# 64-token attention in a float32 network on one core: three one-pass products for q, k and v, and the turned tiles of a layer's last lane issued earlier

## The reference, cut to what matters

```python
def _layer(x, wqkv, qs, ksc, wo, lg, lb, w1, b1, w2, b2):
    h = shift_token(x)                  # upper half of the features moved one token on
    q, k, v = jnp.split(h @ wqkv, 3, axis=-1)         # 128 -> 3 x 512, 8 heads of 64
    q = l2norm(q) * qs
    k = l2norm(k) * ksc
    q, k = rotary_xpos(q, k)
    o = local_attention(q, k, v)        # windows of 64 tokens, each sees itself and the one before
    x = x + o @ wo
    h = layernorm(shift_token(x))
    a, g = jnp.split(h @ w1 + b1, 2, axis=-1)
    return x + (a * gelu(g)) @ w2 + b2
```

## Time and profile before

| | |
|---|---|
| median of the 3 runs | 2840.59 us |
| the profiled execution's own time | 2833.55 us |
| its span | 2831.8 us |
| PE busy | 2659.5 us (94%) |
| DVE, ACT, POOL busy | 1939.5, 1858.8, 1051.8 us (68, 66, 37%) |
| chain that ended last | PE 73%, DVE 11%, ACT 7% |
| granted PE clock, mean | 0.978 |
| the four layers of stage W | 1758.8 to 2225 us and 2360.7 to 2825 us |

### The profile page before, as it was taken

The page is one execution under the profiler, slowest core; times in us unless marked ns, Lnnn a source line. Parts: engine busy times, 40 slices in busy tenths (PEclk is TensorE's granted clock), DMA queues, the critical chain, the costliest instruction groups (busy, mean ns, idle before and its releaser), DMA issues.

```text
span 2831.8 us, 63348 instructions
## 1 busy us (share of the span) xinstructions
PE 2659.5 (94%) x24036; PEld 1812.7 (64%) x24036; DVE 1939.5 (68%) x5616; ACT 1858.8 (66%) x4392; POOL 1051.8 (37%) x876
## 2 busy tenths in 40 slices
PE   8999999999999998899999998998898998998998
PEld 5666656548888885588888885455455563553554
DVE  5555646488788786788888886774675326764774
ACT  5666766626676673478787876776776515875875
POOL 2323323313333330355555552553454013552551
PEclk8999999999999998999999999999999999999999
DMA  1010000000000001000000002210210002111210
GB/s 56 1 43 1 13 1 9 5 9 2 3 2 2 2 2 50 30 2 2 2 2 2 2 2 92 62 45 7 61 49 20 24 1 69 47 30 30 49 42 16
DMA packets 35280, 63.13 MB, mean 22 GB/s; under 512 B 11526, under 2 KB 15654, under 8 KB 33830
## 3 DMA queue, kind: packets, MB, share of 16 engines
q1 hardware_dynamic: 34982, 59.07, 7.5%
HBM read 23.48 MB, written 1.15 MB: 9 GB/s over the span
## 4 chain that ended last, share of the span: by engine, by line
PE 73%; DVE 11%; ACT 7%; issue 3%; SPq 2%; POOL 1%; DMA 1%; DVEq 0%; ACTq 0%; POOLq 0%
PE bank L804 63%; PE bank L1033 5%; PE bank L1153 3%; SPq L770 2%; PE bank L880 1%; ACT low L1364 1%; DVE low L1708 1%; DVE low L1686 1%; ACT work L1400 1%; ACT work L1303 1%; DVE halves L1701 1%; DMA work<-work 1%; DVE work L1588 1%; ACT squared L1275 1%; ACT bank L1279 1%
## 5 line engine op out<-in xcount | busy, mean ns | idle before, releaser
L1271 ACT ACTIVATE low<-bank 128x512 f32<-128x512 f32 (+3 forms) x512 | 427.8, 946 | 0.0
L804 PE MATMUL bank<-table_keys,halves 128*128 128x512 f32 (+3 forms) x1536 | 418.0, 380 | 1.1 <-ACT low L1364 1.0
L804 PE MATMUL bank<-work 128*64 128x128 f32 (+6 forms) x4480 | 364.2, 290 | 39.7 <-DVE work L1795 20.7
L804 PEld LDWEIGHTS bank<-work 128*64 128x64 f32 (+3 forms) x4480 | 265.0, 144 | 211.5 <-issue 147.5
L1364 ACT ACTIVATE low<-bank,low 128x512 f32<-128x512 f32 (+23 forms) x384 | 227.2, 592 | 248.9 <-DVE low L1708 245.4
L1708 DVE TENSOR_REDUCE low<-bank 128x1 f32<-128x512 f32 (+22 forms) x512 | 286.4, 569 | 96.2 <-PE bank L804 91.3
L1898 POOL TENSOR_TENSOR halves<-squared,const 128x512 fp32r<-128x512 f32 x128 | 137.0, 1070 | 510.7 <-PE bank L804 510.7
L1271 ACT ACTIVATE work<-bank 128x512 f32<-128x512 f32 (+4 forms) x389 | 199.5, 538 | 151.2 <-PE bank L804 76.9
L804 PEld LDWEIGHTS bank<-table_keys,halves 128*128 128x128 f32 x1536 | 243.6, 190 | 47.6 <-issue 13.3
L1400 ACT ACTIVATE work<-work 128x192 f32<-128x192 f32 (+1 forms) x512 | 218.7, 431 | 38.2 <-DVE work L1788 38.2
L1947 POOL TENSOR_TENSOR work<-work 128x768 f32<-128x768 f32 x128 | 187.7, 1466 | 135.2 <-DVE work L1799 135.2
(11 more groups left out here) (201 smaller groups left out, 5707.3 us busy)
## 6 DMA issues: line engine op xcount, KB each, us to landing
work<-work SPq DMA_DIRECT2D x512, 64.0 KB, 2.0
slot<-in_wW SPq DMA_DIRECT2D x4, 1605.5 KB, 6.7
slot<-in_wA SPq DMA_DIRECT2D x4, 837.0 KB, 6.4
table_low<-embv_padded SPq DMA_DIRECT2D x2, 1536.0 KB, 6.3
table<-in_dft SPq DMA_DIRECT2D x1, 3072.0 KB, 11.8
slot<-in_wE SPq DMA_DIRECT2D x2, 584.0 KB, 3.7
const<-in_const SPq DMA_DIRECT2D x1, 1094.5 KB, 5.2
squared<-in_x SPq DMA_DIRECT2D x4, 256.0 KB, 6.2
```

Of the source, the lines that this page charges most:

```text
L804: return pe.matmul(o, l, r, start=start, stop=stop)
L1271: return act.activation(dst, src, ACT.Identity)
```

## The change

It does the following.

- q, k and v are now each the sum of three one-pass products: rounded weight times rounded input, rounded weight times the input's rest, and the weight's rest times the rounded input. `w_rotate` and `w_value` issue three `mm` in place of one.
- A new step `w_halves` on POOL, once per layer, makes `W_HI` (copy) and `W_LO` (subtraction) from each of the three 128x512 weights. It stands at the start of each stage W, and for the second layer between the MLPs of lanes 1 and 2 of the layer before.
- A new step `w_split` on POOL, once per lane, makes the rounded input and its rest in `XS` (two buffers). Lane 0's stands right behind its shift, lane 1's in the middle of the head, lane 2's and 3's behind W(j) at the fourth step of lanes 0 and 1.
- `XS` lies in `table_keys`, over the place of the DFT tables; so their load moves from the start of the first stage W to the end of the attention of its second layer (`tables`, which=3).
- In the last lane, from its second step on, `w_turn` of j-1 stands right behind the exponentials of j: PE goes S(j), T(j-1), V(j-2), and DVE goes mask and maximum of j, D(j-1), R(j).

```diff
@@ stage_w
         weights()
+        add("w_halves")
         if seen.get("shift", 0) == 0:
             add("tables", which=2)
-        for c in range(C):
+        add("shift", c=0, via="norm")
+        add("w_split", c=0)
+        for c in range(1, C):
             add("shift", c=c, via="norm")
...
                 if 1 <= j <= lane_items:
                     length(j - 1)
+                if j == lane_items // 2:
+                    add("w_split", c=1)
...
                 if j < len(pairs):
                     add("w_exps", c=lane, i=i, hp=hp)
+                turned = (c >= C - 1 and at > 0)
+                if turned and j <= len(pairs):
+                    lane, i, hp = pairs[j - 1]
+                    add("w_turn", c=lane, i=i, hp=hp)
                 if 2 <= j <= len(pairs) + 1:
...
                     add("w_weigh", c=lane, i=i, hp=hp)
+                if at == 3 and c + 2 < C:
+                    add("w_split", c=c + 2)
                 if c + 1 < C and at in (3, 4, 5, 6):
                     add("w_value", c=c + 1, i=at - 3)
-                if 1 <= j <= len(pairs):
+                if not turned and 1 <= j <= len(pairs):
...
             state["pool"] = range(BANKS)
+            if seen["tables"] == 3 and layer == DEPTH_W - 1:
+                add("tables", which=3)
             add("shift", c=3, via="stream")
...
             if layer < DEPTH_W - 1:
                 weights()
+                add("w_halves")
                 add("shift", c=0, via="stream")
+                add("w_split", c=0)
                 add("w_mlp", c=2, load=load)
...
@@ storage
+        tail = WORK_W - LOW - 6 * T
+        W_HI, W_LO = (halves[:, tail + a * 3 * T:tail + (a + 1) * 3 * T].rearrange("p (x f) -> p x f", x=3) for a in range(2))
+        XS = table_keys[:, 0:4 * T].rearrange("p (l a t) -> p l a t", l=2, a=2)
@@ SP, tables
-                else:
+                elif s.which == 2:
                     sp.wait_ge(sem("r_head_copied"), 2 * BATCHES)
                     sp.dma_start(table[:, 6144:8192], ins["rotary"]).then_inc(sem("rotary_loaded"), 16)
+                else:
+                    sp.wait_ge(sem("w_v_copied"), NT * C * DEPTH_W)
+                    sp.wait_ge(sem("w_squared"), 2 * PAIRS * C * DEPTH_W)
                     sp.dma_start(table[:, 0:6144], ins["dft"]).then_inc(sem("dft_loaded"), 16)
@@ PE, w_rotate
-                pe.wait_ge(sem("shift_done"), C * s.shift + s.c + 1)
-                mm(take(s.k)[:, :], wt(s, WW, s.x, s.pt * P, P), shifted[:, s.c, :]).then_inc(tile_full, 1)
+                layer = s.n // (2 * PAIRS * C)
+                x = "qkv".index(s.x)
+                pe.wait_ge(sem("w_split"), 2 * (C * layer + s.c + 1))
+                pe.wait_ge(sem("w_halved"), 6 * layer + 2 * x + 2)
+                o, mine = take(s.k)[:, :], slice(s.pt * P, s.pt * P + P)
+                mm(o, W_HI[:, x, mine], XS[:, s.c % 2, 0, :], stop=False)
+                mm(o, W_HI[:, x, mine], XS[:, s.c % 2, 1, :], start=False, stop=False)
+                mm(o, W_LO[:, x, mine], XS[:, s.c % 2, 0, :], start=False).then_inc(tile_full, 1)
@@ PE, w_value: the same with XS as the stationary side, 128 columns of it, and W_HI, W_LO moving
@@ POOL
+            def w_halves(s):
+                layer = s.n
+                if layer == 0:
+                    pool.wait_ge(sem("r_head_copied"), 2 * BATCHES)
+                else:
+                    pool.wait_ge(sem("w_v_copied"), NT * C * layer)
+                reached(pool, "w_added", s.rotations)
+                for x, name in enumerate("qkv"):
+                    whole = wt(s, WW, name)
+                    pool.tensor_copy(W_HI[:, x, :], whole).then_inc(sem("w_halved"), 1)
+                    pool.wait_ge(sem("w_halved"), 6 * layer + 2 * x + 1)
+                    pool.tensor_tensor(W_LO[:, x, :], whole, whole_words(W_HI[:, x, :]), ALU.subtract).then_inc(sem("w_halved"), 1)
+                pool.wait_ge(sem("w_halved"), 6 * layer + 6)
+
+            def w_split(s):
+                reached(pool, "w_v_copied", NT * (s.n - 1 if s.c > 1 else s.n - s.c))
+                reached(pool, "w_added", s.rotations)
+                pool.wait_ge(sem("shift_done"), C * s.shift + s.c + 1)
+                pool.tensor_copy(XS[:, s.c % 2, 0, :], shifted[:, s.c, :]).then_inc(sem("w_split"), 1)
+                pool.wait_ge(sem("w_split"), 2 * s.n + 1)
+                pool.tensor_tensor(XS[:, s.c % 2, 1, :], shifted[:, s.c, :], whole_words(XS[:, s.c % 2, 0, :]), ALU.subtract)\
+                    .then_inc(sem("w_split"), 1)
+                pool.wait_ge(sem("w_split"), 2 * s.n + 2)
```

More of the change, by code:

```diff
@@ L604, in hybrid_network @@
         small_w = carve(4, 12)
+        tail = WORK_W - LOW - 6 * T
+        assert cursor[0] <= LOW + tail
+        W_HI, W_LO = (halves[:, tail + a * 3 * T:tail + (a + 1) * 3 * T].rearrange("p (x f) -> p x f", x=3) for a in range(2))
+        XS = table_keys[:, 0:4 * T].rearrange("p (l a t) -> p l a t", l=2, a=2)
         HW = work[:, PAIRS * T:PAIRS * T + 2 * HT_W * T].rearrange("p (a b c) -> p a b c", a=2, b=HT_W)
@@ L1131, in w_value @@
             def w_value(s):
-                mm(take(s.k)[:, :], shifted[:, s.c, s.i * P:(s.i + 1) * P], wt(s, WW, "v")).then_inc(tile_full, 1)
+                layer = s.n // (NT * C)
+                pe.wait_ge(sem("w_split"), 2 * (C * layer + s.c + 1))
+                pe.wait_ge(sem("w_halved"), 6 * layer + 6)
+                o, mine = take(s.k)[:, :], slice(s.i * P, s.i * P + P)
+                mm(o, XS[:, s.c % 2, 0, mine], W_HI[:, 2, :], stop=False)
+                mm(o, XS[:, s.c % 2, 0, mine], W_LO[:, 2, :], start=False, stop=False)
+                mm(o, XS[:, s.c % 2, 1, mine], W_HI[:, 2, :], start=False).then_inc(tile_full, 1)
             def w_scores(s):
@@ L1465, in tables @@
             def tables(s):
-                if s.which == 2:
+                if s.which >= 2:
                     return
@@ L1958, in h_forward @@
                 pool.tensor_tensor(YH[:, b, 1, :], M1[:, b, 1, :], M2[:, b, 0, :], ALU.add).then_inc(sem("h_product"), 1)
-            parts = dict(weights=lambda s: weights_here(pool, s), norm_scale=norm_scale, shift=shift, gate=gate, core=core, a_weigh=a_weigh, w_weigh=w_weigh, w_add=w_add, h_forward=h_forward)
+            parts = dict(weights=lambda s: weights_here(pool, s), norm_scale=norm_scale, shift=shift, w_halves=w_halves, w_split=w_split, gate=gate, core=core, a_weigh=a_weigh, w_weigh=w_weigh, w_add=w_add, h_forward=h_forward)
             pool.wait_ge(sem("const_loaded"), 16)
```

## The result

The changed kernel takes **2860.44 us** in the median of six runs (2846.7 to 2870.62); the kernel before took 2843.67 us in six (2834.72 to 2847.97). The ratio is **1.007**, with an interval of 1.0044 to 1.0096. I had forecast 2841.3 us, no change, in a range of 2824 to 2857: the kernel is slower, by 0.7%, and the time lies outside the range.

A forecast was written before the change was run, and what follows sets the result against it. PE was taken to bound only the main part, loops of waits the head and last lane. Terms -18.4 - 0.5 + 3.2 + 2.8 + 2.4 + 11.2 = +0.7 us on 2840.6 gave 2841.3 us, range 2824 to 2857.

The forecast's parts named there:

- One-pass products, -18.4: Main parts: 144 projections and values each fall by 0.16 us, 23.0 us, of which 80% arrives: -18.4 us.
- Rivals C and D: Product passes: C, each takes 0.86 us, +220 us, chance 0.01; D, quicker passes, some 6 us less, chance 0.08.
- Lane 0's split, +3.2: Start of each stage W: the split delays PE 2.0 us, less 0.4 saved on the first product, twice: +3.2 us.
- lane 1's, +2.8: Head: a 2.0 us split behind an add makes the next add 0.7 us late, four times: +2.8 us.
- lanes 2 and 3, +2.4: Main part: splits between W(j) and the next add cost 0.3 us for each of eight: +2.4 us.
- Rival B: Main part: POOL is late, splits delaying add, scale and ACT; 2.0 us a split, sum +21, 2862 us; chance 0.21.
- w_halves, the DFT load, 0: Start of stage W and between layers: 6 us of halves stay hidden, cover 2 us; the moved table load costs nothing.
- T ahead of V, +11.2: Last lane: T waits for POOL's W, two steps take 6.97 us in place of 6.10; +2.8 us a layer, +11.2 us.
- Rival A: Last lane: the reordering is free or gains; 2830 us, or 2821 us with half the waits recovered; chance 0.25.
- Its eight projections hang on the loop of swap, add and scale, not on PE: 0.: Head: cheaper projections there save no time, since a loop of waits and not PE sets the pace: 0 us.
- if PE's clock falls in the longer gaps, +16: Last lane: upper bound of the reordering's cost, should PE's granted clock fall in its longer gaps: +16 us.
- 7.0 us under the median: Base of the forecast: the profiled execution took 2833.55 us, 7.0 us under the median, so 2840.6 us was used.

The follow-up runs named there:

- e1: The changed kernel with the last lane back in its old order (V before T), all else kept; 2842.94 us, ratio to before 1.0012.
- e3: The changed kernel with the old last-lane order and old float32 products, POOL making halves and splits nobody reads; 2843.32 us, ratio to before 1.0029.
- e2: The kernel before with the last lane's reordering (T ahead of V) and nothing else; 2854.01 us, ratio to before 1.0068.
- e10: The changed kernel with the old last-lane order and two needless float32 products before V(30) in each last lane; 2830.44 us, ratio to before 0.9949.
- e9: The kernel before with two needless float32 products before V(30) in each last lane, nothing else; 2829.11 us, ratio to before 0.9943.
- e5: The changed kernel with the old last-lane order and lane 0's projections and values as float32 products, without its split; 2836.18 us, ratio to before 0.9978.
- e6: The changed kernel with the old last-lane order and lane 0's products given a needless repeat of their first pass; 2838.41 us, ratio to before 0.9991.

## Why the prediction was wrong, point by point

- **One-pass products, -18.4: the size of one product was right, the share that arrives was too high.** 0.89 us a projection against 0.90 forecast, 0.14 us less a value against 0.16. At full clock the first main part gains 3.5 us of 36 x 0.16 = 5.8 us, 60% where I took 80%. Rivals C and D (dearer and quicker passes) fall with these rows. The parts at equal clock say the same: e1 less e3 is -14.6 us, 63% of 23.0.
- **Lane 0's split, +3.2, lane 1's, +2.8, lanes 2 and 3, +2.4.** PE starts 2.1 us later at each of two stages, as forecast, and its first two projections take 2.90 us in place of 3.56. But in e3 the four main parts take 520.3 us (520.1 before) and the heads 112.9 (112.0): in the main part a split costs nothing, in the head 0.2 us a layer in place of 0.7. All of POOL's work is +2.4 us at equal clock; I had 8.4. Rival B (POOL late in the main part, 2862 us) gives the measured time to 2 us by luck: e3 shows its mechanism false.
- **w_halves, the DFT load, 0.** Right: hidden with 1.75 us to spare in the view above, where I had 2.
- **T ahead of V, +11.2.** The loop was right: T 1.78 us behind R, as forecast (R at 1939.47, T at 1941.25), V at once behind T, and POOL as the new releaser. The size is 4.3 us in the first layer's lane, not 2.8. The starts of R give the parts: the first reordered step 1.3 us longer (forecast 1.0), the six behind it 3.0 (forecast 2.6), and the 0.6 us that I gave back at the end did not come (5.6 us from R(31) to the output in either order, at full clock). Four lanes alone are +14.3 us. Rival A (0.25) falls with e2: the reordering is a loss.
- **The sum at an equal clock comes out near** (+2.3 against +0.7), but by luck, since errors cancel: +3.8 on the products, -6.0 on POOL, +3.1 on T.
- **The step that failed is the one on PE's time off the path: "Its eight projections hang on the loop of swap, add and scale, not on PE: 0."** What PE no longer does there was put at nothing, and part of it comes out of the granted clock. The sum had no term for the clock at all; it stood only in a bound of the reordering ("if PE's clock falls in the longer gaps, +16"), and e2 shows 0.001 there. In its place the runs show: the mean fell from 0.975 to 0.967, at 2.28 us per 0.001 some 18 us, which is what the means differ by (20.6) less the 2.3 at equal clock. The one-pass products account for 0.005 to 0.006 of it (e1 against e3, e10 against e9), 12 to 13 us; lane 0's alone, whose projections that sentence is on, for about 0.003 (e5 and e6 against e1), 7 us. POOL's work has 0.001 (e3). Which of the other lanes' products cost the rest, and whether the reordering adds to it once the products are cheap, stays open. A row to start from was before me: the head at 0.87 in the earlier trace rows, the only stretch of the layer well under full clock, with PE busy for 21.7 of 26.0 us.
- **"7.0 us under the median"** was the same thing: the profiled execution had 0.978, 0.003 above the mean of its kernel, 6.9 us on the line.

What stays open: why less busy time in lane 0 also goes with a lower clock at places 100 us later (1.2 GHz behind the last lanes of e1, whose order is that of before). Each profile is one execution, and behind the last lanes the slow stretches do not fall at the same places in each, so these runs do not settle it; only those at the end of the heads stand clear. They too are rarer where the last lanes have the fillers (1.00, 0.81, 1.00 and 1.00 in e10, at the same places as above), and that is as little explained. Not tried either: the old products in lanes 1 to 3 alone, and lane 0's old product with the reordering left in.

## What to carry to other kernels

Time taken from PE where it already waited gained nothing here and was paid for with the clock, so price it by the granted clock of its stretch and of the dense work behind it. Where PE must wait and dense work follows, a needless product placed inside that wait can be worth more than a cheaper product, as here (0.9943 for e9 alone, 1.0012 for e1): try it alone on the kernel before, or its gain is credited to something else. Before an operation is moved ahead of another to end a wait, list what the other one covered (here POOL's 1.47 us under V).

## What the runs showed of the hardware

- The mean granted clock decides between executions of one kernel: the changed kernel's six lie between 2846.7 us at 0.973 and 2870.62 us at 0.963. On the line through them, the clock's 0.010 are 22.8 of these 23.9 us. Most of a difference of 0.3% between executions is this, and it can be read beside each time.
- Eight needless products (two float32 128x512 ones in each of four last lanes, 1.88 us busy a pair) make the kernel before 16 us faster (0.9943).
- POOL's copy of 128x512 took 0.61 us at the start of the stage (shown above), but 1.13 us in the head, where DVE's scale ran beside it; the changed kernel there:

```profile
1777.35 0.69 DVE L1813 SCALAR_TENSOR_TENSOR work<-squared,work 128x512 f32<-128x512 f32 x1 [0.38 <-POOL work L2011]
...
1777.38 1.13 POOL L1930 CAST table_keys<-shifted 128x512 fp32r<-128x512 f32 x1
```

All four heads show it, with copies of 1.07 to 1.13 us that start 0.03 to 0.09 us behind the scale. Where POOL is the first, it is the scale that takes longer; the changed kernel in the second main part:

```profile
2109.80 1.27 POOL L2011 TENSOR_TENSOR work<-work 128x512 f32<-128x512 f32 x1 [1.21 <-DMA work<-work]
...
2109.91 1.71 DVE L1813 SCALAR_TENSOR_TENSOR work<-squared,work 128x512 f32<-128x512 f32 x1
```

I had looked for the contention on DVE's side only. In these rows the one that starts second gives way, and the first keeps its time (0.69 us for the scale, as the median of the earlier trace rows; 1.27 for the add, as in the earlier trace rows). The Trainium skill, "GPSIMD Engine Reference", section Specifications, names the pair of engines and DVE instructions with two SBUF inputs; the trace agrees with the pair, and shows the price of such meetings.
